# Sum over destinations in a graph network stack: loads of column pairs into eight buffers, landings passed on by GpSimd

## Chip, core and metric

The kernel runs on one core of a Trainium2 chip. The metric is the device time of one execution in microseconds (us). TensorE, VectorE, ScalarE and GpSimd (PE, DVE, ACT and POOL in the profile) compute; SyncE (SP) issues most transfers. Each engine runs its own instruction stream and waits on semaphores.

## What is computed

Four graph layers act on a state `x` of 1250 nodes by 768 features. There are 20,000 edges, sorted by destination, each with a relation from 34. The part that the change touches is in the second layer:

```python
agg  = segment_sum(x[src], edge_type * n + dst, num_segments=N_REL * n)
mean = agg / max(cnt, 1)
h1   = einsum('rni,rio->no', mean, W_rel) + x @ W_root + b_rgcn
xw   = h1 @ W_gcn
...            # the degree-normalised sum over edges, as in the other layers
```

The kernel does not form `mean`. It sorts the edges by relation, multiplies the gathered rows by the relation's weights, scales each by 1/count, and stores them in HBM as `messages`, one row of 768 floats per edge, in the order of the destinations. `h1` is then the sum of the messages by destination plus `x @ W_root + b_rgcn`.

## The kernel before

It is written out by hand: one program per engine, semaphores for every dependency, and hardware loops whose bounds are read from small tables that the kernel computes from the edges. The order on each engine is the order of the code.

At the start the edge lists are loaded and turned into `edge` (128 partitions by 160 columns: edge 128*j + p stands in column j, partition p). For each tile of 128 destination nodes VectorE computes the first column that holds one of its edges (`ctl_col`) and how many groups of four columns (a quad, `QUAD` = 4) the tile needs (`ctl_quad`, a running sum). With these inputs the ten tiles have 13, 6, 5, 4, 4, 3, 3, 3, 3 and 2 quads, so 52, 24, 20, 16, 16, 12, 12, 12, 12 and 8 columns, 184 in all. Then come the adjacency matrices, a normalisation, and the first layer's two convolutions (L0a and L0b). After them the relation stage gathers rows, multiplies and scatters `messages`.

The **sum stage** (`sum_tile` on each engine) follows. For tile t:

- TensorE transposes the tile of the state (L1240, from a copy in `rows`), and multiplies it by W_root in 36 products (L1249, `products`). Each fp32 operand is split into a high and a low part in fp32r, and three products of parts are summed.
- For each column j of the tile: SyncE loads 128 message rows into one of four buffers of `w_raw` (L502, 384 KB). ScalarE copies it as its high part into `y_part` (L817). VectorE writes the one-hot matrix of the column's destinations into one of four places of `agg_w` (L1205), and subtracts to get the low part (L1207). TensorE multiplies the one-hot with both parts in two halves, four matmuls into the tile's accumulator (L1417).
- After the last column VectorE adds the bias and writes the tile of `h_act` (L1212), and copies the tile after the next for the transposes (L1199).

The semaphores of a column: `Q.ylow` counts low parts, and the load that reuses a buffer waits for the low part four columns before. `y_land[k]` tells a landing, `Q.yhigh` a high part, and `Q.ymm` TensorE's columns. ScalarE and VectorE wait for `Q.ymm` before they overwrite a place used four columns before. TensorE and VectorE start the counts at `QUAD`, so the first four pass at once. `turn_low` (L856) takes the low part of the transposed tile, `quads` and `bounds` (L357 to L364) read the tables into registers, and `column` turns a quad and its place into j. The next layer's weights are loaded into `w_raw` when the last tile is added.

## Time and profile before

| | us |
|---|---|
| median of 3 runs | 3080.43 (3077.42 to 3080.8) |
| profiled execution, device time | 3085.96 |
| its span | 3084.0 |
| TensorE busy in the span | 2621.4 (85%) |
| VectorE busy | 1604.0 (52%) |
| ScalarE busy | 1126.3 (37%) |
| mean granted TensorE clock | 0.939 of 2.4 GHz |

Busy times are those of single engines, and they overlap. "Idle before" in a row is the time that the engine stood still ahead of the instruction, and the name after the arrow is what ended it. PEld is TensorE's weight load, which is ahead of the matmul that uses it. A line with a q after the engine (PEldq, DVEq) is an instruction of the engine's sequencer: register arithmetic, branches, waits.

### The profile page before, as it was taken

What the parts mean: (1) busy time and instruction counts of PE and PEld (TensorE: products, weight loads), DVE (VectorE), ACT (ScalarE), POOL (GpSimd) and SP (SyncE); (2) the same over time, 40 slices, a digit from 0 to 9 for tenths busy, and PEclk for the clock granted to TensorE, in tenths of its full rate; (3) what the DMA queues carried; (4) which work ended last, traced back from release to release, by engine and by line L of the source; (5) the groups of instructions that cost most, each with busy time, mean ns of one, the idle gap of its engine ahead of it and who ended that gap; (6) DMA issues with size and microseconds to landing.
All of it is one profiled execution on the core that took longest, in us unless ns stands there. A gap on an engine that the chain in (4) does not pass through costs nothing.

```text
span 3084.0 us, 52263 instructions
## 1 busy us (share of the span) xinstructions
PE 2621.4 (85%) x14502; PEld 2425.3 (79%) x14503; DVE 1604.0 (52%) x3028; ACT 1126.3 (37%) x1925; POOL 859.8 (28%) x1207
## 2 busy tenths in 40 slices
PE   0666388976999999999999999677778898987899
PEld 0222188976999999999999999556668887987799
DVE  7765543354344333443334433477764577577734
ACT  0011323232444444444444444355433235446521
POOL 1666610002555555555555555100000000000000
PEclk9987689998999999999999999889989998998999
DMA  3000110124445544555544554577660201001102
GB/s 108 1 1 1 44 47 0 45 86 169 175 174 182 196 174 174 174 188 190 174 174 172 195 188 143 184 239 228 207 199 21 77 25 36 10 13 69 51 21 91
DMA packets 116601, 358.08 MB, mean 116 GB/s; under 512 B 23709, under 2 KB 24177, under 8 KB 116337
## 3 DMA queue, kind: packets, MB, share of 16 engines
q1 hardware_dynamic: 78097, 220.40, 21.2%
q0 software_dynamic: 38464, 137.17, 12.8%
q8 instruction: 23, 0.38, 0.0%
q14 instruction: 17, 0.14, 0.0%
HBM read 267.97 MB, written 93.37 MB: 117 GB/s over the span
## 4 chain that ended last, share of the span: by engine, by line
PE 72%; DVE 11%; issue 5%; ACT 5%; DMA 4%; DVEq 2%; POOL 0%; ACTq 0%; SPq 0%; POOLq 0%
PE ps L1249 50%; PE ps L1304 12%; PE ps L1240 5%; PE ps L1356 4%; DMA w_raw<-messages 3%; DVE xw L1207 1%; PE ps L1417 1%; ACT xw L817 1%; DVE h_act L1115 1%; ACT rows L721 1%; DVE h_act L927 1%; DVEq L1113 1%; PE ps L1362 1%; DVE w_a L850 1%; DVE rows L981 1%
## 5 line engine op out<-in xcount | busy, mean ns | idle before, releaser
L1249 PE MATMUL ps<-w_a,h_t 128*128 128x384 f32 x5580 | 1032.3, 342 | 2.4 <-DVE h_t L856 2.1
L1249 PEld LDWEIGHTS ps<-w_a,h_t 128*128 128x128 f32 x5580 | 982.3, 192 | 6.9 <-DVE h_t L856 4.6
L1304 PE MATMUL ps<-xw,agg_w 128*128 128x384 f32 x2800 | 524.5, 350 | 78.8 <-DVE agg_w L952 47.2
L1304 PEld LDWEIGHTS ps<-xw,agg_w 128*128 128x128 f32 x2800 | 512.6, 197 | 87.7 <-issue 77.1
L1249 PE MATMUL ps<-xw,h_t 128*128 128x384 f32 x3132 | 577.4, 341 | 0.0
L1155 DVE TENSOR_TENSOR h_t<-ps,h_t 128x256 fp32r<-128x256 f32 x516 | 218.7, 424 | 678.5 <-ACT h_t L784 482.3
L1249 PEld LDWEIGHTS ps<-xw,h_t 128*128 128x128 f32 x3132 | 549.0, 188 | 0.0
L784 ACT ACTIVATE h_t<-ps 128x256 fp32r<-128x256 f32 x516 | 198.2, 384 | 677.2 <-PE ps L1249 472.0
L1240 PE MATMUL ps<-ident,rows 128*128 128x128 f32 x1458 | 206.8, 280 | 129.7 <-DVE rows L863 71.2
L636 POOL DMA_INDIRECT messages<-rows,rec_stage x172 | 199.9, 1162 | 354.1 <-ACT rows L778 354.1
L1240 PEld LDWEIGHTS ps<-ident,rows 128*128 128x128 f32 x1458 | 176.4, 144 | 146.3 <-issue 86.1
L599 POOL DMA_INDIRECT h_act<-h_table,rec_stage x175 | 188.7, 1078 | 147.1 <-POOL rec_stage L595 119.4
L1417 PE MATMUL ps<-xw,agg_w 128*128 128x384 f32 x736 | 178.2, 381 | 54.5 <-DVE xw L1207 50.0
L817 ACT ACTIVATE xw<-w_raw 128x768 fp32r<-128x768 f32 x184 | 152.6, 843 | 167.3 <-DMA w_raw<-messages 91.2
L1417 PEld LDWEIGHTS ps<-xw,agg_w 128*128 128x128 f32 x736 | 134.7, 206 | 95.9 <-DVE xw L1207 94.5
L1356 PE MATMUL ps<-h_act 128*128 128x512 bf16 x552 | 151.0, 393 | 63.1 <-DVE h_act L1115 53.6
L604 POOL DMA_INDIRECT w_at<-inv_table,rec_stage x175 | 182.9, 1045 | 61.4 <-issue 61.4
L1207 DVE TENSOR_TENSOR xw<-w_raw,xw 128x768 fp32r<-128x768 f32 x184 | 176.0, 957 | 44.4 <-ACT xw L817 43.7
L575 POOL DMA_INDIRECT records<-rec_stage x157 | 158.4, 1009 | 128.4 <-POOL rec_stage L571 121.7
L856 DVE TENSOR_TENSOR h_t<-ps,h_t 128x256 fp32r<-128x256 f32 x213 | 86.9, 423 | 185.6 <-ACT h_t L664 184.2
L1356 PEld LDWEIGHTS ps<-h_act 128*128 128x128 bf16 x552 | 43.4, 105 | 173.8 <-DVE h_act L1115 133.2
L664 ACT ACTIVATE h_t<-ps 128x256 fp32r<-128x256 f32 x183 | 70.2, 385 | 295.8 <-PE ps L1249 206.1
(183 smaller groups left out, 2188.8 us busy)
## 6 DMA issues: line engine op xcount, KB each, us to landing
w_raw<-in_L_gnn_W_rel SPq DMA_DIRECT2D x68, 1152.0 KB
w_raw<-messages SPq DMA_DIRECT2D x184, 384.0 KB, 3.8
rows<-x_state SPq DMA_DIRECT2D x50, 384.0 KB, 3.0
w_raw<-in_L_gnn_W SPq DMA_DIRECT2D x10, 1152.0 KB
x_state<-rows SPq DMA_DIRECT2D x30, 384.0 KB, 2.3
h_table<-h_act SPq DMA_DIRECT2D x10, 384.0 KB, 2.4
x_state<-in_x SPq DMA_DIRECT2D x1, 3750.0 KB, 14.2
out<-rows SPq DMA_DIRECT2D x9, 384.0 KB
```

Source lines behind the costliest of these rows:

```text
L599: pool.indirect_dma_start(out=x_ring[:, k, :], out_offset=None, in_=h_table, in_offset=bass.IndirectOffsetOnAxis(gather_at[:, k, 0:1], 0)) ...
L604: pool.indirect_dma_start(out=w_at[:, k:k + 1], out_offset=None, in_=inv_table, in_offset=bass.IndirectOffsetOnAxis(gather_at[:, k, 1:2], ...
L636: pool.indirect_dma_start(out=messages, out_offset=bass.IndirectOffsetOnAxis(scatter_at[:, k, :], 0), in_=rows[:, 2 + u, :], in_offset=Non ...
L784: act.activation(h_t[:, 0, 2 * g:2 * g + 2, :], turn_group(g).rearrange("p (k n) -> p k n", k=2), ACT.Copy)\
L817: act.activation(y_part[:, 0, k, :], w_raw[:, k, :], ACT.Copy).then_inc(Q.yhigh, 1)
L1155: dve.tensor_tensor(h_t[:, 1, 2 * g:2 * g + 2, :], turn_group(g).rearrange("p (k n) -> p k n", k=2), h_t[:, 0, 2 * g:2 * g + 2, :].bitcast ...
L1207: dve.tensor_tensor(y_part[:, 1, k, :], w_raw[:, k, :], y_part[:, 0, k, :].bitcast(F32), ALU.subtract)\
L1240: ins = pe.transpose(turn_out(k), tile[:, k * P:(k + 1) * P], ident[:])
L1249: ins = pe.matmul(acc(h), h_t[:, a, k, :], w[:, b, k, h * HF:(h + 1) * HF], start=(k == 0 and a == 0 and b == 0), stop=(stop and k == KB - ...
L1304: ins = pe.matmul(ps[:, 2 + 2 * u + h, 0:wide], agg_w[:, a, b, :], xw[:, c, b, h * HF:h * HF + wide], start=first, stop=last, skip_group_c ...
L1356: ins = pe.matmul(ps_flat[:, lo:hi], oh[:, k % 2, 0:P], oh[:, k % 2, P + lo:P + hi], start=False, stop=True, skip_group_check=True)
L1417: ins = pe.matmul(rel_acc(t)(h), agg_w[:, 0, k, :], y_part[:, b, k, h * HF:(h + 1) * HF], start=False, stop=True, skip_group_check=True)
```

## The change

In the sum stage:

- `w_raw` and `rows` become two parts of one tensor `land`, whose first eight rows of 768 floats are the landing buffers `y_ring`. `y_part` has eight places (`LAND` = 8) for each part. One load brings two columns (`PAIRS` = 4 loads in a round of eight columns).
- SyncE no longer follows the tiles: it loops over pairs of quads and reads each quad's first column from a table `quad_col`. The number of such pairs stands in `ctl_half[1]`. A load waits for the low parts of the two columns that were in its buffers, eight before.
- `quad_columns`, new on VectorE ahead of the relation stage, computes this table of 400 entries on one partition.
- GpSimd, after the relation stage, waits for each landing in turn and increments `Q.yready`. ScalarE waits for this count.
- ScalarE may be eight columns ahead of TensorE. The one-hots stay with VectorE and in four places: the counts start at `LAND`, and VectorE's wait is for four more than before.
- The places in `y_ring` and `y_part` are chosen by q % 2, a register value, where they were constants.
- The copy for the transposes of this stage goes to `rows[:, 2]`.

Elsewhere: six semaphores of the preparation become two counters, two become `x_ready`, and the rows of `messages` behind the last edge are zeroed with other shapes.

```diff
@@ constants, tensors
+LAND = 2 * QUAD
+PAIRS = LAND // 2
+    message_rows = messages[0:ECP * P, :].rearrange("(c p) d -> p c d", c=ECP)
-        w_raw = sb("w_raw", [P, KB, D], F32)
+        land = sb("land", [P, KB + 4, D], F32)
+        w_raw, rows = land[:, 0:KB, :], land[:, KB:KB + 4, :]
+        y_ring = land[:, 0:LAND, :]
-        rows = sb("rows", [P, 4, D], F32)
-        y_part = xw[:, :, 0:QUAD, 0:D]
+        y_part = xw[:, :, 0:LAND, 0:D]
+        quad_col = rec_out[0:1, :, :].rearrange("p c w -> p (c w)")[:, 0:QMAX]
+        quad_acc, quad_step = rows[0:1, 2, 0:QMAX], rows[0:1, 3, 0:QMAX]
+        def landed(q, k):
+            return y_ring[:, ds(q % 2 * QUAD + k, 1), :].rearrange("p a d -> p (a d)")
+        def part(a, q, k):
+            return y_part[:, a, ds(q % 2 * QUAD + k, 1), :].rearrange("p a d -> p (a d)")
@@ SyncE
-            at = E
-            while at < ECP * P:
-                n = min(ECP * P - at, 3 * 80)
-                sp.dma_start(messages[at:at + n, :].rearrange("(p r) d -> p r d", r=3), zero_rows[0:n // 3, :, :])\
-                  .then_inc(zeroed, 16)
-                at += n
+            sp.dma_start(message_rows[:, EC:ECP, :], zero_rows)\
+              .then_inc(x_ready, 16)
+            sp.dma_start(message_rows[ELAST:P, EC - 1:EC, :], zero_rows[ELAST:P, 0:1, :]).then_inc(x_ready, 16)
...
-            with sp.Fori(0, NT) as t:
-                q0, q1, c0 = quads(sp, t)
-                with sp.Fori(q0, q1) as q:
-                    for b in range(QUAD):
-                        j = column(c0, q, q0, b)
-                        sp.wait_ge(Q.ylow, q * QUAD + b + 1)
-                        sp.dma_start(w_raw[:, b, :], messages[ds(j * P, P), :])\
-                          .then_inc(y_land[b], 16)
+            pairs = sp.value_load(ctl_half[0:1, 1:2], min_val=1, max_val=QMAX // 2)
+            with sp.Fori(0, pairs) as i:
+                for u in range(2):
+                    j = sp.value_load(quad_col[0:1, ds(2 * i + u, 1)], min_val=0, max_val=ECP - QUAD)
+                    for b in range(2):
+                        k = 2 * u + b
+                        sp.wait_ge(Q.ylow, i * LAND + (2 * k + 2))
+                        sp.dma_start(y_ring[:, 2 * k:2 * k + 2, :], message_rows[:, ds(j + 2 * b, 2), :]).then_inc(y_land[k], 16)
+            for k in range(PAIRS):
+                sp.wait_ge(y_land[k], pairs * 16)
+                sp.sem_inc(turn_taken, 1)
@@ GpSimd, after the relation stage
+            pairs = pool.value_load(ctl_half[0:1, 1:2], min_val=1, max_val=QMAX // 2)
+            with pool.Fori(0, pairs) as i:
+                for k in range(PAIRS):
+                    pool.wait_ge(y_land[k], i * 16 + 16)
+                    pool.sem_inc(Q.yready, 1)
@@ ScalarE, sum_tile
-                        act.wait_ge(y_land[k], q * 16 + 16)
+                        act.wait_ge(Q.yready, q * 2 + (k // 2 + 1))
                         act.wait_ge(Q.ymm, q * QUAD + (k + 1))
-                        act.activation(y_part[:, 0, k, :], w_raw[:, k, :], ACT.Copy).then_inc(Q.yhigh, 1)
+                        act.activation(part(0, q, k), landed(q, k), ACT.Copy).then_inc(Q.yhigh, 1)
@@ VectorE
+            def quad_columns():
+                q_first, q_base, q_delta = att[0:1, 0, :], att[0:1, 1, :], seg_max[0:1, 0, :]
+                dve.wait_ge(R.addr, 1)
+                dve.tensor_copy(q_first, ctl_quad[0:1, 0:NT])
+                link(dve.tensor_copy(q_base, ctl_col[:]))
+                link(dve.scalar_tensor_tensor(q_base, q_first, -float(QUAD), q_base, ALU.mult, ALU.add))
+                dve.tensor_copy(q_delta[:, 0:1], q_base[:, 0:1])
+                dve.tensor_tensor(q_delta[:, 1:NT], q_base[:, 1:NT], q_base[:, 0:NT - 1], ALU.subtract)
+                link(dve.tensor_scalar(quad_acc, iota_n[0:1, 0:QMAX], float(QUAD), None, ALU.mult))
+                for t in range(NT):
+                    link(dve.tensor_scalar(quad_step, iota_n[0:1, 0:QMAX], q_first[:, t:t + 1], q_delta[:, t:t + 1],
+                                           ALU.is_ge, ALU.mult))
+                    link(dve.tensor_tensor(quad_acc, quad_acc, quad_step, ALU.add))
+                dve.tensor_scalar(mv[0:1, 0:1], ctl_quad[0:1, NT:NT + 1], 1.0, None, ALU.add)
+                link(dve.tensor_scalar(quad_col, quad_acc, float(ECP - QUAD), None, ALU.min))
+                link(dve.tensor_copy(ctl_half[0:1, 1:2], mv[0:1, 0:1]))
+                link(dve.tensor_scalar(ctl_half[0:1, 1:2], ctl_half[0:1, 1:2], 1, None, ALU.arith_shift_right))
+            quad_columns()
             dve.wait_ge(R.ready, 1)
...
-            dve.sem_inc(Q.ylow, QUAD)
+            dve.sem_inc(Q.ylow, LAND)
...
-                        dve.wait_ge(Q.ymm, q * QUAD + (k + 1))
+                        dve.wait_ge(Q.ymm, q * QUAD + (k + 1 + QUAD))
                         dve.tensor_scalar(agg_w[:, 0, k, :], iota_n[:, ds(t * P, P)], edge[:, 1, ds(j, 1)], None, ALU.is_equal)
                         dve.wait_ge(Q.yhigh, q * QUAD + (k + 1))
-                        dve.tensor_tensor(y_part[:, 1, k, :], w_raw[:, k, :], y_part[:, 0, k, :].bitcast(F32), ALU.subtract)\
+                        dve.tensor_tensor(part(1, q, k), landed(q, k), part(0, q, k).bitcast(F32), ALU.subtract)\
                            .then_inc(Q.ylow, 1)
@@ TensorE
-            pe.sem_inc(Q.ymm, QUAD)
+            pe.sem_inc(Q.ymm, LAND)
...
-                        pe.wait_ge(Q.ylow, q * QUAD + (k + 1 + QUAD))
+                        pe.wait_ge(Q.ylow, q * QUAD + (k + 1 + LAND))
                         for b in range(2):
                             for h in range(2):
-                                ins = pe.matmul(rel_acc(t)(h), agg_w[:, 0, k, :], y_part[:, b, k, h * HF:(h + 1) * HF],
+                                ins = pe.matmul(rel_acc(t)(h), agg_w[:, 0, k, :], part(b, q, k)[:, h * HF:(h + 1) * HF],
                                                 start=False, stop=True, skip_group_check=True)
```

On TensorE two columns of a quad in `sum_tile`'s inner loop stood like this (`xw` holds `y_part`, `sum_ylow` is `Q.ylow`, ISA is a register or wait instruction of the sequencer):

```order
L1417 MATMUL ps<-xw,agg_w 128x384 [waits sum_ylow]
L1417 MATMUL ps<-xw,agg_w 128x384 x3
L1414 REGISTER_ALU
L1417 MATMUL ps<-xw,agg_w 128x384 [waits sum_ylow]
L1417 MATMUL ps<-xw,agg_w 128x384 x3
```

and one column of the changed kernel, at the same place, stands like this:

```order
L1452 ISA [waits sum_ylow]
L1452 MATMUL ps<-xw,agg_w 128x384
L1452 ISA
L1452 MATMUL ps<-xw,agg_w 128x384
L1452 ISA
L1452 MATMUL ps<-xw,agg_w 128x384
L1452 ISA
L1452 MATMUL ps<-xw,agg_w 128x384
L1449 REGISTER_ALU
```

Each of the four matmuls of a column now has a sequencer instruction ahead of it, and the column's wait stands on the first of these.

On VectorE a column of the same loop stood so, the one-hot and the subtraction (`sum_ymm` is `Q.ymm`, `sum_yhigh` is `Q.yhigh`):

```order
L1205 ISA [waits sum_ymm]
L1205 ISA
L1205 TENSOR_SCALAR agg_w<-iota_n,edge 128x128
L1207 TENSOR_TENSOR xw<-w_raw,xw 128x768 [waits sum_yhigh]
L1204 REGISTER_ALU
```

and now:

```order
L1240 ISA [waits sum_ymm]
L1240 ISA
L1240 TENSOR_SCALAR agg_w<-iota_n,edge 128x128
L1241 REGISTER_ALU
L1242 ISA [waits sum_yhigh]
L1242 ISA
L1242 TENSOR_TENSOR xw<-land,xw 128x768
L1239 REGISTER_ALU
```

Three sequencer instructions have come between the one-hot and the subtraction.

On SyncE, which issues the loads, the inner loop of two columns stood so:

```order
L502 ISA [waits sum_ylow]
L502 DMA w_raw<-messages 128x768
L501 REGISTER_ALU
L502 ISA [waits sum_ylow]
L502 DMA w_raw<-messages 128x768
```

and half a round of the new loop, one quad, so:

```order
L505 TENSOR_LOAD rec_out
L505 ISA x2
L508 ISA
L509 ISA [waits sum_ylow]
L509 DMA land<-messages 128x2x768
L508 REGISTER_ALU
L509 ISA [waits sum_ylow]
L509 DMA land<-messages 128x2x768
```

A quad now takes two loads instead of four and one table read of its own (`quad_col` lies in `rec_out`); the reads of `ctl_quad` and `ctl_col` once a tile are gone.

## Rows read from the trace of the kernel before

**Rows 1.** The page, part 1: busy time, share of the span, instructions.

```profile
PE 2621.4 (85%) x14502; PEld 2425.3 (79%) x14503; DVE 1604.0 (52%) x3028; ACT 1126.3 (37%) x1925; POOL 859.8 (28%) x1207
```

**Rows 2.** Groups by line, 1966 to 2298 us: busy, mean ns, idle before.

```profile
L1207 DVE TENSOR_TENSOR xw<-w_raw,xw 128x768 fp32r<-128x768 f32 x184 | 176.0, 957 | 44.4 <-ACT xw L817 43.7
L817 ACT ACTIVATE xw<-w_raw 128x768 fp32r<-128x768 f32 x184 | 152.6, 843 | 167.3 <-DMA w_raw<-messages 91.2 <-PE ps L1417 70.8 <-issue 1.9
```

**Rows 3.** Waits, 1966 to 2298 us: total, times, longest.

```profile
PEld ps L1417 <- DVE xw L1207: 94.5, 122, 1.8
ACT xw L817 <- DMA w_raw<-messages: 91.2, 109, 2.4
...
DVE agg_w L1205 <- PE ps L1417: 30.8, 10, 4.8
```

**Rows 4.** Timeline of VectorE, 2049 to 2070 us: start, duration, instruction, idle before.

```profile
2051.77 0.96 DVE L1212 TENSOR_TENSOR h_act<-ps,rows 128x768 f32 x1 [1.36 <-PE ps L1417]
...
2063.05 0.29 DVE L1205 TENSOR_SCALAR agg_w<-iota_n,edge 128x128 fp32r x1 [3.69 <-PE ps L1417]
2063.58 0.96 DVE L1207 TENSOR_TENSOR xw<-w_raw,xw 128x768 fp32r<-128x768 f32 x1 [0.24 <-ACT xw L817]
...
2064.65 0.95 DVE L1207 TENSOR_TENSOR xw<-w_raw,xw 128x768 fp32r<-128x768 f32 x1
```

**Rows 5.** Timeline of TensorE and its weight loads, second and fourth tile.

```profile
2053.89 8.08 PE L1249 MATMUL ps<-w_a,h_t 128*128 128x384 f32 x36
...
2061.63 3.61 PEld L1417 LDWEIGHTS ps<-xw,agg_w 128*128 128x128 f32 x20
2065.66 0.65 PEld L1417 LDWEIGHTS ps<-xw,agg_w 128*128 128x128 f32 x4 [0.41 <-DVE xw L1207]
...
2131.15 6.49 PE L1249 MATMUL ps<-w_a,h_t 128*128 128x384 f32 x36
```

**Rows 6.** Timeline of VectorE, first restart, end of the second tile, last addition.

```profile
1978.23 0.29 DVE L1205 TENSOR_SCALAR agg_w<-iota_n,edge 128x128 fp32r x1 [4.18 <-PE ps L1417]
...
2091.28 0.95 DVE L1207 TENSOR_TENSOR xw<-w_raw,xw 128x768 fp32r<-128x768 f32 x1
...
2093.61 0.96 DVE L1212 TENSOR_TENSOR h_act<-ps,rows 128x768 f32 x1 [0.39 <-PE ps L1417]
...
2296.10 0.96 DVE L1212 TENSOR_TENSOR h_act<-ps,rows 128x768 f32<-128x768 f32 x1 [1.06 <-PE ps L1417]
```

**Rows 7.** Stretches: length, busy by engine, TensorE clock, DMA share, GB/s.

```profile
1963.00:1964.00 1.00, 0.00 (x0) 0.00 (x0) 0.00 (x0) 0.00 (x0) 0.00 (x0) 0.50 1.03 402
...
1975.00:1976.00 1.00, 1.00 (x8) 1.00 (x7) 0.00 (x0) 0.00 (x0) 0.00 (x0) 1.00 0.87 304
...
1978.00:2048.00 70.00, 49.97 (x195) 35.98 (x193) 53.36 (x95) 39.70 (x48) 0.00 (x0) 0.90 0.79 247
```

**Rows 8.** DMA issues of the stage: KB each, median us to landing.

```profile
w_raw<-messages SPq DMA_DIRECT2D x184, 384.0 KB, 3.8
```

**Rows 9.** Sequencer instructions of lines: min/median/max ns, first and last start.

```profile
L1414 PEldq ALU_OP  x3: 32/32/36, 2287.1 to 2287.7; - x3
...
L1249 PEldq FUSED_REGOPS  x362: 60/91/136, 743.7 to 2257.4; - x181
...
L1205 DVEq FUSED_REGOPS  x228: 52/158/231, 1969.3 to 2293.0; - x114
```

**Rows 10.** Timeline, 725 to 742 us: GpSimd and VectorE.

```profile
725.89 0.11 POOL L589 MEMSET rows<- 128x10 int32 x1 [320.95 <-DMA h_table<-h_act]
...
740.90 0.56 DVE L1167 COPY rows<-h_act 128x768 f32<-128x768 f32 x1 [18.50 <-POOLq L612]
```

**Rows 11.** Timelines of VectorE at the start and in the first layer.

```profile
48.04 0.18 DVE L1068 TENSOR_SCALAR rows<-rows 128x34 f32<-128x34 f32 x1
48.26 0.19 DVE L1069 TENSOR_TENSOR rows<-rows 128x33 f32<-128x33 f32 x1
...
721.72 0.68 DVE L915 TENSOR_SCALAR h_act<-rows,mv 128x768 f32<-128x768 f32 x1
```

More of the change, by code:

```diff
@@ L338, in gnn_stack @@
         Q = SumSems(sem)
-        y_land = [sem(f"y_land{b}") for b in range(QUAD)]
+        y_land = [sem(f"y_land{b}") for b in range(PAIRS)]
         block = ctx.enter_context(nc.Block())
@@ L1198, in sum_tile @@
                     dve.wait_ge(Q.turned, KG * t + KG)
-                    dve.tensor_copy(rows[:, 0, :], tile_rows(h_act, t + 1)).then_inc(Q.copied, 1)
+                    dve.tensor_copy(rows[:, 2, :], tile_rows(h_act, t + 1)).then_inc(Q.copied, 1)
                 q0, q1, c0 = quads(dve, t)
@@ L1328, in _ @@
                 ins = pe.transpose(ps[:, 1, a * 32:(a + 1) * 32], float_b[:, a, :], ident[0:32, 0:32])
-            ins.then_inc(pre.turned, 1)
-            pe.wait_ge(pre.extremes, 1)
-            pe.transpose(ps[0:2 * NT, 2, 0:P], small[:, 0, 0:2 * NT], ident[:]).then_inc(pre.extremes_turned, 1)
-            pe.wait_ge(pre.best, 1)
+            ins.then_inc(pre.pe_step, 1)
+            pe.wait_ge(pre.dve_step, 1)
+            pe.transpose(ps[0:2 * NT, 2, 0:P], small[:, 0, 0:2 * NT], ident[:]).then_inc(pre.pe_step, 1)
+            pe.wait_ge(pre.dve_step, 2)
             pe.matmul(ps[0:1, 3, 0:2 * NT], small[0:2 * NT, 1, 0:1], ident[0:2 * NT, 0:2 * NT], start=True, stop=True)\
-              .then_inc(pre.row, 1)
-            pe.wait_ge(pre.tot, 1)
+              .then_inc(pre.pe_step, 1)
+            pe.wait_ge(pre.dve_step, 3)
             own = small[:, 3, 0:NR]
             pe.matmul(ps[:, 4, 0:NR], before[:], own, start=True, stop=True, skip_group_check=True)
-            pe.matmul(ps[:, 4, 64:64 + NR], ones[:], own, start=True, stop=True, skip_group_check=True).then_inc(pre.prefix, 1)
+            pe.matmul(ps[:, 4, 64:64 + NR], ones[:], own, start=True, stop=True, skip_group_check=True).then_inc(pre.pe_step, 1)
             cuts = [(0, 512), (512, 1024), (1024, NP + NR)]
@@ L1397, in _ @@
             pe.wait_ge(w_low, 2 * (w_no["root"] + 1))
-            pe.sem_inc(Q.ymm, QUAD)
+            pe.sem_inc(Q.ymm, LAND)
             pe.wait_ge(Q.copied, 1)
-            turn(Q, rows[:, 0, :])
+            turn(Q, rows[:, 2, :])
             def sum_tile(t, more):
@@ L1405, in sum_tile @@
                     pe.wait_ge(Q.copied, t + 2)
-                    turn(Q, rows[:, 0, :])
+                    turn(Q, rows[:, 2, :])
                 pe.wait_ge(Q.ofree, t + 1)
```

43 lines of the change are left out of this document (19 added, 24 removed).

## Prediction

> **What bounds the kernel now.** I read the page's first part, then by stretch. Over the whole span TensorE is busy for 85% [rows 1], but the diff works in one stage, the sum over destinations, which runs here from about 1960 to 2297 us. In that stage the groups by line and the waits show something else than the page: TensorE, VectorE and ScalarE all wait in turn. ScalarE's split L817 waits 91.2 us for landings of column loads, TensorE's weight load waits 94.5 us for VectorE's low part L1207, and VectorE's one-hot waits 30.8 us in ten pieces for TensorE [rows 2, 3]. Followed back: TensorE waits for VectorE, VectorE for ScalarE, ScalarE for a load whose buffer was freed only four columns before.
>
> The timeline of VectorE shows two kinds of time. When columns have landed, low parts follow each other every 1.07 us (2063.58, 2064.65): a one-hot and a subtraction. After a tile's last column comes a pause of another kind: the addition to `h_act`, the copy for the next transposes, four columns ahead, and then a stop until TensorE has done the root products and one column; for the second tile it runs from 2051.77 to 2063.05 [rows 4]. TensorE itself needs only 0.72 us for a column at 2.4 GHz (20 weight loads, so five columns, in 3.61 us) and 6.5 us for the root products, 8.1 us when part of them falls on 1.2 GHz [rows 5].
>
> So there are 184 columns, and three rates: VectorE 1.07 us, TensorE 0.72 us, and what the loads give. From the first restart of VectorE (1978.23) to the last addition (2296.10) are 317.9 us [rows 6]. The nine pauses from a tile's addition to the next restart, 7.8 to 12.4 us long, make 94.3 us of it (the first is that of [rows 4], 11.3). The other 223.6 us are column stretches, and in them loads set the rate: 1.48 us a column in the first tile of 52.
>
> **The change part by part.**
>
> *Eight landing and eight part buffers, loads of pairs.* Loads run eight columns ahead, ScalarE eight columns ahead of TensorE. The one-hots still have four places, and the wait for them is shifted so that it remains "TensorE has done the column four before". The pauses therefore stay as they are, and a column stretch becomes VectorE's own pace if loads keep up. A tile of n columns then takes, from its restart: 0.2 us to the first subtraction, (n-5) times 1.066, and 2.33 from the last subtraction's start to the addition (2091.28 to 2093.61, a tile whose last columns ran at 2.4 GHz) [rows 6]. The tiles have 52, 24, 20, 16, 16, 12, 12, 12, 12 and 8 columns, so n-5 adds up to 134: 134 x 1.066 + 10 x 2.53 = 168.1 us. Against 223.6 that is a gain of **55.4 us**, 20.9 of it in the first tile.
>
> *Do the loads keep up?* One column is 393 KB. With loads queued behind each other the engines moved 402 GB/s, 0.98 us a column; four single loads spaced by VectorE got 304 GB/s, 1.29 us; the present stretch 247 GB/s at a DMA share of 0.79, which is latency (median 3.8 us to landing, four buffers) more than rate [rows 7, 8]. Pairs, four of them in the queue, stand between the first two; I take 1.15 us. In the first tile that is 48 x (1.15 - 1.066) = 4.0 us, against at least four columns landed when the stretch starts, so 0 to 4: I take 2. At 1.29 it is 48 x 0.22 = 10.8 less some 4.3 of store, and little in the 24-column tile: 7. At 0.98 nothing. The Trainium skill ("DMA: Bandwidth & Descriptors", section Measured) puts a 1 MB transfer at 341 GB/s, and the section on 436 GB/s sees an HBM limit of about 358 per core. By those a column would take 1.10 to 1.15 us, loads and not VectorE would be the pace, and the first tile would lose 1.6 to 4 us, by an estimate from that page. The trace's 402 GB/s is above it.
>
> *Slots addressed by register.* ScalarE, VectorE and TensorE now compute addresses before each instruction. On VectorE one such step takes 0.05 to 0.23 us, median 0.16 [rows 9]. In the steady state they run while a 0.96 us subtraction does, and three or four of them fit into 1.066. Only at a restart nothing covers the two ahead of the subtraction: 0.2 us ten times, **-2.0 us**. On TensorE four steps come per column. Its sequencer passed three columns' loop steps between 2287.1 and 2287.7, some 0.3 us for four weight loads and matmuls [rows 9]. A step of TensorE's costs 0.06 to 0.14 us, median 0.09 [rows 9], so a column needs 0.3 + 4 x 0.09 = 0.66 us of sequencer, still under 0.72. At 0.136 it is 0.84, still under 1.066. What is exposed is the first step after each release, at a tile's last column: 0.15 us ten times, **-1.5 us**. ScalarE has 0.84 us of work against 1.066 and is ahead by up to eight.
>
> *GpSimd passes landings on.* One more semaphore step per pair. From the end of a low part (2064.65 + 0.95) to TensorE's weight load at 2065.66 are 0.06 us [rows 4, 5], so the hop costs about 0.1 to 0.2 us in landing time. GpSimd has nothing else left to do then, and with a pair in store it is hidden: 0. If loads set the pace it lies in their loop of eight columns and is worth 0.02 us a column.
>
> *The table of columns.* `quad_columns` puts 29 small instructions on VectorE ahead of the relation stage, released by the memset at 725.89; VectorE would start there at 740.90 [rows 10]. Nothing of 1 x 400 elements is in the trace. Scaling between 33 and 768 elements, a tensor-tensor goes from 0.19 to 0.96, so 0.57 at 400; a tensor-scalar from 0.18 to 0.68, so 0.43 [rows 11, 2]. Ten pairs with 0.04 between are 10.8 us, the rest some 2.3: 13.1 us in a gap of 14.9. The cover is GpSimd's records load and first gather. If every tensor-scalar cost as much as a tensor-tensor it would be 14.8: 0. If an instruction took 20% more than that, 3 us would be exposed on the chain (TensorE idles there too).
>
> *The rest.* Fewer semaphores and another cut of the zeroing at the start: the same 480 rows, waited for hundreds of microseconds later: 0. The load of the next weights still follows the last addition. The first loads are now eight columns behind the load of `h_act`; with one queue in order that load is not later.
>
> *TensorE's clock.* In the first stretch its mean grant is 0.90 [rows 7]: short spells at 1.2 GHz while it waits much. With a column per 1.07 us instead of 1.48 it waits less. The five slow pauses of 11.2 us or more could come down to the 9.7 of the fast ones (up to +9 us); against it, a spell at 1.2 GHz inside a stretch, where a column takes about 1.37 us, now costs 0.3 us a column, where loads covered it before. I take **+2 us**.
>
> Sum: 55.4 - 2.0 - 2.0 - 1.5 + 2 = 51.9. The profiled execution took 3085.96 us (span 3084.0), so 3034 for it; the median of the runs shown is 5.5 us lower, 3080.43, so I forecast **3029 us**.
>
> **The rivals.**
>
> *Loads set the pace* (0.16). If pairs get no more than 1.4 to 1.5 us a column, as the stretch does now, the first tile costs some 20 - 5, the next two 4 more: 20 us off the sum, gain 32, 3048. For it: today's 247 GB/s at a share of 0.79. Against it: 402 GB/s while queued.
>
> *TensorE's instruction stream becomes the pace* (0.09). If a column needs c of sequencer above 0.95 us, the stage takes 184 c + 86.8 (94.3 less ten times 0.75 for what lies between TensorE's first column and VectorE's restart). At c = 1.19 (0.147 per matmul and 0.15 per step) that is 305.8 against 317.9: gain 12, 3068. Against it: 0.3 us for four matmuls now.
>
> *Slower* (0.03). The same mechanism on the other side: it decides from c = 1.256, that is 0.31 us for each matmul with its address step. At c = 1.4 the stage takes 344 us, 27 more: 3107. The Trainium skill ("TensorE: Matmul & The Clock Gate", section "Wait — 56ns, not 53.3ns?") gives about 62 ns a matmul where ucode decodes it. The row's pace for weight load and matmul together agrees roughly with that, so this stays small.
>
> *It does not do what it says* (0.03): the four one-hot places tie VectorE to TensorE, so buffers behind them could be worth nothing, 3080. Against it: the one-hot waits only 30.8 us, all of it in the pauses [rows 3].
>
> *More than forecast* (0.07): no shortfall of loads and all pauses fast, gain 60 to 64, 3017 to 3020.
>
> **How the numbers follow.** My forecast, VectorE's pace with a gain of 42 to 60, has 0.62; its own range is 3020 to 3039. The range of 3017 to 3054 adds the higher gain and loads as the pace, and leaves out about 0.15. Slower by over 0.2% is 0.03, within 0.2% 0.03 (about what a measurement of this kernel can tell from no change), faster 0.94.
>
> **What would show it.** In the changed profile: ScalarE's wait for landings falls from 91 to under 15 us, low parts every 1.07 us from restart to tile end, waits of VectorE for TensorE still ten and some 30 us, first tile 53 to 58 us instead of 73.5, the last addition near 2244. Steps within TensorE's column: weight loads of a column in 0.65 us as now; if they spread to 1 us or more, the forecast is wrong by the second rival. If landings still release ScalarE in the first tile, it is the first. VectorE starting the relation stage later than 740.9 would show the table exposed.

## The result, and the profile after

| | before | after |
|---|---|---|
| median | 3080.61 us | 3038.27 us |
| ratio after to before (95% interval) | | 0.9861 (0.9842 to 0.988) |
| profiled execution | 3085.96 us | 3035.31 us |
| span | 3084.0 us | 3033.2 us |
| granted TensorE clock, mean | 0.939 | 0.943 |

One more execution of each kernel was disturbed and some 800 to 1000 us longer; the ratio leaves both out, and without them the medians are 3080.43 and 3038.12 us. The change makes the kernel 1.4% faster: 42.3 us by the medians and 50.7 us between the two profiled executions. Forecast were 3029 us, and a range of 3017 to 3054 that holds the result; it lies at the upper edge of the main forecast's own range, 3020 to 3039. The difference between 42 and 51 is itself a part of the answer, below.

The groups by line of the sum stage of the changed kernel, 1960 to 2262 us (line, engine, instruction, busy us, mean ns, idle before and what ended it). They answer to [rows 2]; the one-hot is now L1240, the low part L1242, ScalarE's split L832, TensorE's column L1452.

```profile
L1242 DVE TENSOR_TENSOR xw<-land,xw x184 | 175.6, 954 | 9.0 <-ACT xw L832 5.5 <-issue 0.4
L1452 PE MATMUL ps<-xw,agg_w 128*128 x736 | 167.5, 357 | 20.4 <-DVE xw L1242 9.6
L832 ACT ACTIVATE xw<-land x184 | 144.7, 837 | 119.9 <-POOLq L660 85.1 <-PE ps L1452 33.8 <-issue 0.8
L1452 PEld LDWEIGHTS ps<-xw,agg_w 128*128 128x128 f32 x736 | 121.9, 188 | 64.5 <-issue 64.4
...
L1240 DVE TENSOR_SCALAR agg_w<-iota_n,edge 128x128 fp32r (+1 forms) x184 | 51.9, 282 | 40.6 <-PE ps L1452 22.2 <-issue 18.3
```

The subtraction takes what it took, 954 ns. What has gone is the idle time around it: VectorE waits 5.5 us for ScalarE in the whole stage, ten times (before 43.7). Two rows must be read with care. ScalarE still waits 85.1 us for landings, nearly as long as before, but now it stands up to eight columns ahead, and only those 5.5 us of it reach VectorE. And TensorE's weight load no longer shows "VectorE" as the end of its 64.4 us but "issue": its wait for the low part stands on the register step ahead of the first weight load now, and the profile can't follow a semaphore through that.

VectorE's timeline in the first tile (start, duration, instruction, idle before):

```profile
1989.91 0.96 DVE L1242 TENSOR_TENSOR xw<-land,xw  x1
1990.78 0.28 DVE L1240 TENSOR_SCALAR agg_w<-iota_n,edge 128x128 fp32r x1
1990.98 0.95 DVE L1242 TENSOR_TENSOR xw<-land,xw  x1
1991.85 0.28 DVE L1240 TENSOR_SCALAR agg_w<-iota_n,edge 128x128 fp32r x1
1992.49 0.96 DVE L1242 TENSOR_TENSOR xw<-land,xw  x1 [0.36 <-ACT xw L832]
```

Low parts start 1.07 us apart, as forecast, and now and then one is late because its pair hasn't landed: seven waits of 0.27 to 0.75 us in this tile. The first eight steps behind the restart are all 1.07 us, and the ninth is the first late one; from there to the end of the tile the mean is 1.19 us. The first restart and the last addition, for the length of the stage, and the first tile's end with the restart behind it:

```profile
1976.28 0.29 DVE L1240 TENSOR_SCALAR agg_w<-iota_n,edge 128x128 fp32r x1 [4.15 <-PE ps L1452]
...
2034.06 0.96 DVE L1247 TENSOR_TENSOR h_act<-ps,land 128x768 f32 x1 [0.46 <-PE ps L1452]
...
2045.37 0.29 DVE L1240 TENSOR_SCALAR agg_w<-iota_n,edge 128x128 fp32r x1 [3.48 <-PE ps L1452]
...
2242.72 0.96 DVE L1247 TENSOR_TENSOR h_act<-ps,land 128x768 f32<-128x768 f32 x1 [1.17 <-PE ps L1452]
```

From 1976.28 to 2242.72 are 266.4 us. The stage before took 317.9, and 317.9 less the forecast gain of 51.9 is 266.0. Cut as in the prediction: nine pauses of 88.0 us together (before 94.3) and ten stretches of 178.5 (before 223.6). The first tile takes 57.8 us instead of 73.5. The tiles of 8, 12 and 16 columns take 5.74, 10.3 and 14.6 us, with no wait for a load in them.

TensorE's register steps, in the sequencer's rows (ns: shortest, median, longest), answer to [rows 9]:

```profile
L1452 PEldq FUSED_REGOPS  x736: 46/46/120, 1973.8 to 2242.0; - x184
```

and the table, VectorE from the memset on:

```profile
724.23 0.11 POOL L598 MEMSET land<- 128x10 int32 x1 [321.71 <-DMA h_table<-h_act]
...
725.37 0.47 DVE L1173 TENSOR_SCALAR land<-iota_n,att,seg_max 1x400 f32<-1x400 uint16 x1
725.88 0.56 DVE L1175 TENSOR_TENSOR land<-land 1x400 f32<-1x400 f32 x1
...
737.08 0.14 DVE L1179 TENSOR_SCALAR ctl_half<-ctl_half 1x1 int32<-1x1 int32 x1
739.95 0.56 DVE L1202 COPY land<-h_act 128x768 f32<-128x768 f32 x1 [2.73 <-POOLq L621]
```

It ends 12.8 us after it started (forecast 13.1, with 29 instructions where there are 30), and VectorE then waits 2.73 us for the first gather: the table is hidden. The relation stage starts 15.7 us after the memset, before it was 15.0 [rows 10]. The difference of 0.7 us was 0.5 between x_before and x_after. VectorE waits for GpSimd in all four profiles, so the table doesn't end that wait, and why GpSimd is later is not shown.

### The profile page after: what moved, and what is told of

Same layout as the page of the kernel before. It is cut to its first block, busy times and chain, and to the rows that moved or that the text cites. A ratio compares the mean times of both kernels' runs of the same rounds, so it can differ in the third digit from the quotient of the medians.

```text
span 3033.2 us, 53789 instructions
## 1 busy us (share of the span) xinstructions
PE 2610.2 (86%) x14502; PEld 2412.2 (80%) x14503; DVE 1604.6 (53%) x3058; ACT 1118.5 (37%) x1925; POOL 857.5 (28%) x1207
## 4 chain that ended last, share of the span: by engine, by line
PE 76%; DVE 10%; ACT 4%; issue 4%; DMA 2%; DVEq 2%; POOL 1%; ACTq 0%; SPq 0%; POOLq 0%
PE ps L1284 51%; PE ps L1339 12%; PE ps L1275 5%; PE ps L1391 4%; PE ps L1452 3%; DMA land<-messages 1%; DVE h_act L1130 1%; DVE h_act L942 1%; ACT land L736 1%; PE ps L1397 1%; DVE w_a L865 1%; DVEq L1128 1%; DVE land L996 1%; DVE land L955 1%; DVE xw L1242 0%
## 5 line engine op out<-in xcount | busy, mean ns | idle before, releaser
L1339 PE MATMUL ps<-xw,agg_w 128*128 128x384 f32 x2800 | 528.7, 351 | 78.3 <-DVE agg_w L967 47.0
L1339 PEld LDWEIGHTS ps<-xw,agg_w 128*128 128x128 f32 x2800 | 516.8, 198 | 87.2 <-issue 77.4
L1275 PE MATMUL ps<-ident,land 128*128 128x128 f32 x1458 | 206.9, 280 | 129.7 <-DVE land L878 70.8
L645 POOL DMA_INDIRECT messages<-land,rec_stage x172 | 200.3, 1164 | 349.3 <-ACT land L793 349.3
L1275 PEld LDWEIGHTS ps<-ident,land 128*128 128x128 f32 x1458 | 177.3, 144 | 143.8 <-issue 57.8
L832 ACT ACTIVATE xw<-land x184 | 144.7, 837 | 119.9 <-POOLq L660 85.1
L1452 PE MATMUL ps<-xw,agg_w 128*128 x736 | 167.5, 357 | 20.4 <-DVE xw L1242 9.6
L1242 DVE TENSOR_TENSOR xw<-land,xw x184 | 175.6, 954 | 9.0 <-ACT xw L832 5.5
L1452 PEld LDWEIGHTS ps<-xw,agg_w 128*128 128x128 f32 x736 | 121.9, 188 | 64.5 <-issue 64.4
```

What stands on the lines that cost most here:

```text
L645: pool.indirect_dma_start(out=messages, out_offset=bass.IndirectOffsetOnAxis(scatter_at[:, k, :], 0), in_=rows[:, 2 + u, :], in_offset=Non ...
L1242: dve.tensor_tensor(part(1, q, k), landed(q, k), part(0, q, k).bitcast(F32), ALU.subtract)\
L1275: ins = pe.transpose(turn_out(k), tile[:, k * P:(k + 1) * P], ident[:])
L1339: ins = pe.matmul(ps[:, 2 + 2 * u + h, 0:wide], agg_w[:, a, b, :], xw[:, c, b, h * HF:h * HF + wide], start=first, stop=last, skip_group_c ...
L1452: ins = pe.matmul(rel_acc(t)(h), agg_w[:, 0, k, :], part(b, q, k)[:, h * HF:(h + 1) * HF], start=False, stop=True, skip_group_check=True)
```

## The experiments

All kernels are edits of the changed kernel unless said otherwise. Each ratio is against executions of before taken beside it. Their median was 3082.52 us beside x_before, x_after, x_ahead4 and x_single, 3085.88 beside x_hop, x_table2, x_hot8 and x_quad, and 3080.92 beside x_ahead6, x_single4 and x_hot8_single, so medians of different groups are compared only to a few us. "Stage", "pauses" and "stretches" are cut as above, from the profiled execution of each. "Pace" is that of the first tile, (its time - 2.83) / 47: the 2.83 us are what a tile takes besides the n - 5 columns (0.42 from the restart to the first low part and 2.41 from the last one's start to the addition). For before it is 2.6. Where one-hots have eight places VectorE doesn't stop after four columns, and the stage is counted from the fifth one-hot all the same.

**x_before, x_after: both kernels again.** No edit.

> The kernel before, profiled a second time. Theory A (the first profiled execution stood some 5 us above the median because TensorE's clock fell more often in the pauses between tiles): this one takes about 3080, and its nine pauses of the sum stage add up to 86 to 91 us instead of 94.3; the column stretches stay at 220 to 225 us. Theory B (the 5 us were spread over the whole span, outside the stage): pauses again 94 us, and the stage from first restart to last addition again 318 us.

> The changed kernel again, with more rounds. If the stage's gain of 51.5 us between the two profiles is the gain of the change, the time is 48 to 52 us under the kernel before; if part of it was the first profile of the kernel before, 40 to 46 us under it. Stage 264 to 270 us from first restart to last addition.

Before again: 3077.98 us, stage 308.1, pauses 86.3, stretches 221.8. After again: 3037.51 us, ratio 0.9845 (0.9825 to 0.9865), stage 266.2, pauses 86.3, stretches 179.9. Between these two profiled executions the whole difference is 40.5 us and that of the stage 41.9, all of it in stretches. So in the first profile of before 8 us were slow pauses that another execution does not have, and the change does nothing to pauses.

**x_single: eight single loads.** One load per column, each with its own semaphore; GpSimd passes on each.

```diff
-                        sp.wait_ge(Q.ylow, i * LAND + (2 * k + 2))
-                        sp.dma_start(y_ring[:, 2 * k:2 * k + 2, :], message_rows[:, ds(j + 2 * b, 2), :]).then_inc(y_land[k], 16)
+                        sp.wait_ge(Q.ylow, i * LAND + (k + 1))
+                        sp.dma_start(y_ring[:, k:k + 1, :], message_rows[:, ds(j + b, 1), :]).then_inc(y_land[k], 16)
```

> The changed kernel with eight loads of one column each in the eight places instead of four pairs. Theory 1 (depth): first tile within 3 us of the changed kernel's 57.8, time within 4 us of it; perhaps a little better, since a place is refilled one column earlier. Rival (pairs raise the rate of the loads): first tile 62 to 70 us, time 6 to 20 us slower than the changed kernel.

3029.64 us, ratio 0.9824 (0.9809 to 0.984). Stage 259.2, pauses 88.0, stretches 171.2, first tile 52.9. That is neither of the expected cases: singles are 7.9 us faster than x_after, outside the 4 us of the first theory, and the rival had the wrong sign. The rows of the stage, and below them the stretch 1985 to 2017 us (busy by engine, then clock, DMA share, GB/s):

```profile
L1242 DVE TENSOR_TENSOR xw<-land,xw x184 | 174.8, 950 | 3.3 <-ACT xw L832 0.4 <-issue 0.3
...
1985.00:2017.00 32.00, 29.09 (x122) 19.62 (x122) 32.00 (x61) 23.93 (x29) 0.00 (x0) 1.00 0.99 358
```

VectorE is busy for all 32 us and waits 0.4 us for ScalarE in the stage: this is VectorE's pace without a shortfall, 1.065 us a column. So the forecast's figure for a stage with loads that keep up is right (its 168.1 us plus 3.0 of register steps, below), and pairs cost 8.7 us of stretches against singles (179.9 to 171.2).

**x_quad: two loads of four columns**, the other way.

```diff
+                    sp.wait_ge(Q.ylow, i * LAND + (QUAD * u + QUAD))
+                    sp.dma_start(y_ring[:, QUAD * u:QUAD * u + QUAD, :], message_rows[:, ds(j, QUAD), :]).then_inc(y_land[u], 16)
```

> The changed kernel with two loads of four columns (1.5 MB each) in a round of eight instead of four pairs. Theory (rate is not the limit, the loop from a freed place to its landing is): coarser refills make the store give out earlier: first tile 60 to 72 us, 4 to 20 us slower. Rival (larger loads move at the 400 GB/s of queued ones and that is what limits): first tile 53 to 57 us and 2 to 6 us faster.

3083.58 us, ratio 0.9992 (0.9982 to 1.0002). Stage 309.5, stretches 220.2, first tile 74.8: eight buffers as in the change, and the whole gain is gone, far more than the 4 to 20 us expected. VectorE's timeline and the same stretch:

```profile
1989.77 0.96 DVE L1240 TENSOR_TENSOR xw<-land,xw  x1 [3.94 <-ACT xw L830]
...
1995.72 0.96 DVE L1240 TENSOR_TENSOR xw<-land,xw  x1 [1.59 <-ACT xw L830]
...
2002.06 0.96 DVE L1240 TENSOR_TENSOR xw<-land,xw  x1 [1.99 <-ACT xw L830]
```

```profile
1985.00:2017.00 32.00, 21.62 (x77) 17.30 (x77) 20.86 (x39) 15.23 (x20) 0.00 (x0) 0.77 0.75 260
```

Four columns come at once and then VectorE waits 2 us, every 6.3 us. The DMA engines are busy for 75%, not full.

**x_ahead4, x_ahead6, x_single4: the ring held to fewer columns.** The load waits for a low part four, two and four columns later; the last with single loads.

```diff
-                        sp.wait_ge(Q.ylow, i * LAND + (2 * k + 2))
+                        sp.wait_ge(Q.ylow, i * LAND + (2 * k + 2 + 4))    # x_ahead4; x_ahead6: + 2
-                        sp.wait_ge(Q.ylow, i * LAND + (k + 1))            # of x_single
+                        sp.wait_ge(Q.ylow, i * LAND + (k + 1 + 4))        # x_single4
```

> The changed kernel with loads let out only four columns ahead of the low parts, still in pairs and in eight places. Theory 1 (the gain is the depth of eight columns in landing buffers): the gain is lost and more, since two pairs in flight are coarser than four single loads: first tile 72 to 85 us, time 0 to 25 us above the kernel before. Rival (the gain comes from pairs, fewer issues, or from ScalarE and the parts being eight deep): the first tile stays under 65 us and most of the 42 us remain.

> Pairs as in the change, each waiting for a low part two columns later: six columns ahead instead of eight. With four ahead the stretches took 299.6 us, with eight 179.9. Theory A (a ring turns in a fixed time from a freed pair to its landing and split, so the pace is that time over the columns ahead; from four ahead: 98.4 / 52 = 1.89 us a column, 7.6 us a turn, of which six ahead would give 1.26): first tile 63 to 68 us, stretches 195 to 210, 3055 to 3070 us. Rival B (the 8 us that pairs cost at eight ahead is a loss at the tile's start, not a pace, and six ahead is still enough): stretches 180 to 186, 3037 to 3044 us.

> Single loads, but each waits for a low part four columns later, so that only four columns are ahead as in the kernel before; the eight places, register steps, the pass through GpSimd and the table stay. Theory A (the gain of the change is the depth of the load ring and nothing else; the other parts cost next to nothing): stretches 220 to 226 us as before (221.8), pauses 86 to 90, 3078 to 3086 us. Rival B (part of the gain comes from elsewhere, for instance from fewer semaphores or ScalarE's eight part buffers): stretches under 215 us, under 3070. Rival C (the hop and the register steps, which eight columns of store hide, show once the loads set the pace): four columns per turn of the ring and 0.1 to 0.3 us a turn more, 46 turns: stretches 226 to 236, 3086 to 3096.

x_ahead4: 3158.36 us, ratio 1.0252 (1.0236 to 1.0267), stage 387.9, stretches 299.6, first tile 98.4: 76 us over before, where 0 to 25 were expected. x_ahead6: 3071.89 us, 0.9975 (0.9962 to 0.9988), stretches 209.8, first tile 66.1, in the expected window but for a time just above it. x_single4: 3090.33 us, 1.0034 (1.002 to 1.0047), stretches 233.8, first tile 76.2, which is the third of its cases. From x_single it differs in the wait alone, and this is worth 62.6 us of stretches (233.8 to 171.2): the depth of the ring is the gain. The 12 us over x_before's 221.8, 0.26 us per turn of four columns, are what the pass through GpSimd, the register steps and the new loop on SyncE cost together when loads set the pace; they were not taken apart. With eight single loads none of it is seen.

Median times from a load's issue to its landing, in the issue rows of x_single, x_single4, x_ahead6, the changed kernel and x_quad, in this order (each from its own profile):

```profile
land<-messages SPq DMA_DIRECT2D x184, 384.0 KB, 4.5
```

```profile
land<-messages SPq DMA_DIRECT2D x184, 384.0 KB, 3.8
```

```profile
land<-messages SPq DMA_DIRECT2D x92, 768.0 KB, 4.6
```

```profile
land<-messages SPq DMA_DIRECT2D x92, 768.0 KB, 5.4
```

```profile
land<-messages SPq DMA_DIRECT2D x46, 1536.0 KB, 6.5
```

Put together, after the runs, one relation fits all of them roughly. A load of g columns in a ring of A is issued when the *last* of its g places is free, and lands as a whole for its *first* column. That leaves it A - g + 1 columns of lead (landing times of before and of x_ahead4 are from issue rows not shown, that of x_after is from its own profile, not the one above):

| kernel | A | g | lead, columns | pace, us a column | landing, us |
|---|---|---|---|---|---|
| x_ahead4 | 4 | 2 | 3 | 2.03 | 4.4 |
| before (x_before) | 4 | 1 | 4 | 1.50 | 3.8 |
| x_single4 | 4 | 1 | 4 | 1.56 | 3.8 |
| x_quad | 8 | 4 | 5 | 1.53 | 6.5 |
| x_ahead6 | 6 | 2 | 5 | 1.35 | 4.6 |
| the change (x_after) | 8 | 2 | 7 | 1.18 | 5.7 |
| x_single | 8 | 1 | 8 | 1.065, VectorE's | 4.5 |

In a steady ring, lead times pace less the subtraction's 0.96 us must cover landing and split. For x_ahead6 that is 5 x 1.35 - 0.96 = 5.8 us against 4.6 + 0.84 = 5.4; for before 5.0 against 4.6, for x_ahead4 5.1 against 5.2, for x_quad 6.7 against 7.3, for x_single4 5.3 against 4.6. It is an estimate to 0.8 us. For x_after it gives (5.7 + 0.84 + 0.96) / 7 = 1.07 us, right at VectorE's 1.066, so that every late pair shows; measured were 1.18. For eight singles it gives 0.79, and a late load is covered. Lead alone doesn't order the kernels: x_quad has 5 columns and is no faster than before with 4; its loads take 6.5 us to land and not 3.8. Nor is the landing time a constant of the load: the same pairs land in 4.4 us with four columns ahead, in 4.6 with six and in 5.4 to 5.7 with eight.

**x_hop: the pass through GpSimd made longer.** Two reads of the table between landing and increment.

```diff
                     pool.wait_ge(y_land[k], i * 16 + 16)
+                    pool.sem_inc(turn_taken, 1)
+                    for _ in range(2):
+                        pool.value_load(ctl_half[0:1, 1:2], min_val=1, max_val=QMAX // 2)
                     pool.sem_inc(Q.yready, 1)
```

> The changed kernel with two table reads on GpSimd between each landing and its increment, about 1 us more for every pair. Theory (the hop lies in the loop of loads only where the store of landed columns has run out): 10 to 12 us of delay do not show in the short tiles; the first tile grows by 3 to 8 us and the time by 4 to 12 us. Rival (the hop is on every pair's path): 92 times 1 us in part, 40 us or more. Rival (the hop is nowhere on the path): within 2 us.

The sequencer's rows of that line give the price of one read:

```profile
L662 POOLq FUSED_REGOPS  x176: 147/147/152, 1980.0 to 2250.8; - x176
L662 POOLq SEQ_ASSERT  x176: 18/18/18, 1980.1 to 2251.0; - x176
L662 POOLq TENSOR_LOAD <-ctl_half x175: 282/286/305, 1980.2 to 2250.5; - x175
```

Two of 0.45 us are 0.90 us more per pair. 3053.36 us, ratio 0.9899 (0.9878 to 0.9919). Stretches 187.9 against 179.9: 8.0 us, 4.1 in the first tile, whose pace goes from 1.177 to 1.264. With a lead of 7 the relation above gives 0.90 / 7 = 0.13, and 0.09 were found. So where loads are tight a column pays for the pass, but less than a seventh of its delay. In the changed kernel GpSimd's own step for a pair is one wait of 17 ns:

```profile
L660 POOLq EVENT_SEMAPHORE  x92: 17/17/17, 1963.8 to 2234.5; - x92
```

What a semaphore's way from one engine to the next adds is not in this row. At the 0.1 to 0.2 us of the prediction the pass would cost 1 to 2 us of stretches, an estimate by the 8.0 us for 0.90. With 1.7 us of pauses the stage is 9.8 us longer than x_after's; the medians are 15.8 us apart, 12.5 if each is taken from before beside it, where 4 to 12 were expected. Another 6 us of the profiled executions lie in the relation stage (first restart less relation start is 1239.9 us here, 1234.0 in x_after), whose code is the same; the kernels with four one-hot places have 1233.6 to 1240.0 there, so I take it as that stage's own spread; its cause is not shown. The profiled execution won back 3.5 us elsewhere.

**x_table2: the table computed twice.**

```diff
             quad_columns()
+            quad_columns()
```

> The changed kernel with the table of columns computed twice, 12.8 us more of VectorE ahead of the relation stage. Theory (the first 12.8 us are covered with some 2.7 us to spare): the relation stage starts about 10 us later and the time grows by 9 to 11 us. Rival (what was covered is only partly so): 12 to 13 us. Rival (the cover is longer than the idle row shows): under 6 us.

3051.99 us, ratio 0.9887 (0.9867 to 0.9907), 14.5 us over x_after, or 11.1 if each is taken from before beside it (33.9 under it, x_after 45.0); expected were 9 to 11. The relation stage starts 26.0 us after the memset and not 15.7:

```profile
752.24 0.14 DVE L1179 TENSOR_SCALAR ctl_half<-ctl_half 1x1 int32<-1x1 int32 x1
752.42 0.56 DVE L1203 COPY land<-h_act 128x768 f32<-128x768 f32 x1
```

With two tables VectorE goes on without a wait, and what stands beyond the old start is lost whole: 10.3 us. The single table had 2.7 us of cover left. The profiled execution (3056.43 us) is 18.9 us over x_after's: the others are 6.0 in the relation stage and 3.4 in pauses, both of which vary with the execution.

**x_hot8: the one-hots in eight places too.** `hot_place` picks one of eight by q % 2; VectorE waits for TensorE's column eight before. TensorE takes one of two bodies with fixed addresses, by q % 2.

```diff
-                        dve.wait_ge(Q.ymm, q * QUAD + (k + 1 + QUAD))
-                        dve.tensor_scalar(agg_w[:, 0, k, :], ...)
+                        dve.wait_ge(Q.ymm, q * QUAD + (k + 1))
+                        dve.tensor_scalar(hot_place(q, k), ...)
@@ TensorE
+                    with pe.If(q % 2 < 1):
+                        quad_products(0)
+                    with pe.If(q % 2 > 0):
+                        quad_products(1)
```

> The changed kernel with one-hots in eight places as well: VectorE's wait is then for TensorE's column eight before; TensorE chooses between two written-out quads by a branch, so its addresses are constants. Theory (the pauses are TensorE's root products plus VectorE standing still after four columns): VectorE's 22 us of waits for TensorE go, and 1.9 to 4.2 us a tile are gained, less where the loads give out earlier: 10 to 20 us faster than the changed kernel, 3018 to 3028. Rival (loads set the pace once VectorE works through the pause): under 6 us faster, and ScalarE's waits for landings grow by what VectorE's waits shrink.

3019.21 us, ratio 0.9795 (0.9776 to 0.9814). The stage is 253.8 us, 12.4 shorter than x_after's: pauses 69.4 instead of 86.3, stretches 184.4 instead of 179.9. VectorE spends less time standing, and the loads have less time to build up a store; with single loads the stretches don't grow (next run). The medians are 18.3 us apart, so some 6 us of that are not in the stage as it is counted here, where each of the restarts is set at the fifth one-hot.

**x_hot8_single: both.**

> The eight single loads and the eight places of the one-hots together. Theory A (the two act on different things: single loads bring the column stretches to VectorE's pace, eight one-hot places take the wait for TensorE out of the pauses): the stage from VectorE's first restart to the last addition takes 69 us of pauses plus about 175 to 177 of stretches, 244 to 247, and the run 3009 to 3014 us, some 8 below eight places with pairs (3019.2). First tile 53 to 55 us. Rival B (once the one-hots run ahead, VectorE or TensorE's register steps and not the loads make the 4.9 us by which those stretches were longer than with four places): stretches stay at 182 to 185, 3017 to 3020 us.

3007.12 us, ratio 0.9762 (0.974 to 0.9783), the fastest kernel of the study: 2.4% under before. Stage 240.4, pauses 69.5, stretches 170.9; the two act apart, as the first theory had it, and the stage comes out below its 244. From 1985 to 2017 us its DMA engines moved 363 GB/s at a share of 1.00, so little is left there for a faster VectorE:

```profile
1985.00:2017.00 32.00, 29.03 (x127) 20.44 (x126) 32.00 (x62) 24.71 (x30) 0.00 (x0) 1.00 1.00 363
```

A pause of this kernel, VectorE:

```profile
2027.77 0.96 DVE L1251 TENSOR_TENSOR h_act<-ps,land 128x768 f32 x1 [0.36 <-PE ps L1457]
2028.65 0.55 DVE L1238 COPY land<-h_act 128x768 f32 x1
2031.21 0.29 DVE L1244 TENSOR_SCALAR agg_w<-iota_n,edge  x1 [2.01 <-issue]
2031.50 0.96 DVE L1246 TENSOR_TENSOR xw<-land,xw  x1
...
2034.70 0.96 DVE L1246 TENSOR_TENSOR xw<-land,xw  x1
2035.57 0.28 DVE L1244 TENSOR_SCALAR agg_w<-iota_n,edge  x1
2035.77 0.95 DVE L1246 TENSOR_TENSOR xw<-land,xw  x1
```

In [rows 4] VectorE stopped after four columns until TensorE was through with the root products. Here it goes on with the fifth, at 2035.57. The 2.01 us ahead of the first one-hot stay; they are the loop bounds of the next tile, read from the tables.

## Why the prediction was right, and where it was not

**What sets the pace: right.** VectorE at 1.07 us a column wherever columns have landed, its waits for TensorE in the pauses left as they were (22.2 us in nine here and 20.0 in nine in x_after, 30.8 in ten in the first profile of before and 22.5 in ten in x_before), TensorE's own stream not in the way. A column's four weight loads take 0.65 us as before, and one register step 46 ns at the median, not 0.09 us:

```profile
1979.94 0.65 PEld L1452 LDWEIGHTS ps<-xw,agg_w 128*128 128x128 f32 x4 [0.41 <-issue]
```

TensorE's weight loads stand idle for 0.41 us between two columns. That rules out the second rival and the slower one, which both needed a stream above 0.95 us a column. "It does not do what it says" fell with the result.

**Exposed register steps (-2.0 and -1.5): right in sum, 3.0 us.** The short tiles have no load in their way and show it: 5.74 us for 8 columns and 10.30 for 12 are 0.42 + (n - 5) x 1.066 + 2.41 to 0.3 us. Forecast without the steps were 0.2 and 2.33. So a tile costs 0.3 us more, ten of them 3.0, of the 3.5: 0.22 at the restart (forecast 0.2) and 0.08 at the end (forecast 0.15). The 0.2 was a steady column's figure and not one of a restart. Before took 0.53 from restart to subtraction, 0.24 of it a wait for ScalarE [rows 4], and the changed kernel takes 0.42.

**Do the loads keep up (-2): the step that failed.** The stretches came to 178.5 us. Less 134 x 1.066 + 28.3 = 171.1 that is 7.4 us of shortfall, 4.9 of it in the first tile, 1.3 in each of the next two. x_single, with a shortfall of 0.1, shows that it comes from the loads. The forecast took a cost per column from rates, and its 1.15 us was nearly met: the first tile's pace here is 1.17 (57.78 less 2.83, over 47). What was mis-sized is what it took off. It let the store halve the first tile's 4.0 us, and it put the two tiles behind at nothing, which cost 2.6 us. The store did carry eight steps, and the pace behind it was 1.19. The rival of loads at 1.4 to 1.5 us a column, as before, did not come.

That the 1.15 was close is luck in part, since it was read from rates. The 402 GB/s of a full queue stood in a stretch of 1 us, and no 32 us listed here have more than 363. From 1985 to 2017 us eight singles move 358 GB/s at a DMA share of 0.99 and pairs 334 at 0.96; from 1977 to 2009 both have a share of 0.88, singles 313 and pairs 299 GB/s. The changed kernel's two stretches, and below them x_single's of 1977 to 2009:

```profile
1977.00:2009.00 32.00, 27.28 (x116) 18.61 (x115) 30.07 (x56) 18.91 (x25) 0.00 (x0) 1.00 0.88 299
1985.00:2017.00 32.00, 26.23 (x109) 17.57 (x108) 29.32 (x55) 20.81 (x27) 0.00 (x0) 1.00 0.96 334
...
1977.00:2009.00 32.00, 29.48 (x129) 20.94 (x128) 29.91 (x56) 21.61 (x26) 0.00 (x0) 1.00 0.88 313
```

These shares don't tell whether the engines could have done more for pairs. x_hop does in part: 0.90 us of delay that moves no bytes costs 0.09 us a column, some 0.6 us of the seven columns' lead, so the time from a freed pair to its landing is for the most part what sets the pace. The lead explains it: a pair waits for its second place and holds up its first column, and x_quad, at a share of 0.75, takes that to where nothing of the gain is left. That the size of the load plays a part beside the lead is not excluded: no run holds single loads to a lead of 7. The value for "at 1.29" in the prediction, 7, is what it came to, by another way. The Trainium skill ("DMA: Bandwidth & Descriptors", section Measured) gives larger transfers the higher rate, for transfers issued from GpSimd, and by it singles should have been the slowest form. Here, with rings of the same eight buffers and loads issued from SyncE, it was the other way: 358 GB/s with 384 KB, 334 with 768 KB, 260 with 1.5 MB, all from 1985 to 2017 us.

**TensorE's clock and the pauses (+2): right in sign for the first pair of profiles, and nothing in general.** Between those the pauses came down by 6.3 us. x_before had 86.3 us of pauses without the change, x_after 86.3 with it. The slow pauses of 11.2 us and more (two in the changed kernel's profile, five in before's) come and go with the execution, so the sign was luck. The spells at 1.2 GHz inside a stretch that were set against it did not come in the part looked at: the granted clock is 1.00 from 1977 to 2017 us.

**From the profile to the median: the other term that was off.** The forecast of 3034 us for the profiled execution was missed by 1.3 us; in the stage a shortfall of 5.4 more was made up by 4.3 of pauses and 0.5 of steps, so that nearness is luck. Then 5.5 us were taken off, since the profiled execution of before was that much above its median. But part of what made it longer were five slow pauses, and the changed kernel's execution had only two. Reckoned to typical executions, the gain is 55.4 - 7.4 - 3.0, less the 1.8 by which x_before's stretches were shorter than the first profile's: 43.2 us, and 41.9 were found in the stage. The runs don't resolve more: the five later runs put the ratio at 0.9825 to 0.9865, which is 42 to 54 us.

**The table and the pass through GpSimd (0 and 0): right**, both by cover. The table's 12.8 us are hidden with 2.7 to spare and would cost in full behind that (x_table2). Nothing is seen of the pass with eight single loads; with pairs it may be worth 1 to 2 us (estimate, x_hop), and together with the register steps and SyncE's loop it is 12 us when only four columns are ahead (x_single4).

**ScalarE's wait for landings: a wrong sign to look for.** "Under 15 us" was expected and 85.1 came. The engine runs ahead of what it feeds, so its wait says only that it is the faster one. What it passes on is VectorE's wait for it, 5.5 us. In x_single, where no load is short, ScalarE still waits 68.5 us for landings and VectorE 0.4 for ScalarE.

## What to carry to other kernels

Reckon a ring of buffers by its lead, ring size less columns per load plus one, times the pace of the consumer, and hold that against the time from issue to landing plus the steps behind it: a bigger load in the same ring takes lead away, and small loads with enough in flight can be the faster ones. The landing time has to be that of the ring reckoned with, since it grew here with the columns in flight. When an engine ahead of the pace-setter waits, follow the wait to the next engine before counting it as a loss. And before a gain in waits is forecast from one profile, see whether another execution has these waits at all.

## What the runs showed of the hardware that was not expected

- A matmul whose operand's place is picked by a register has a step of 46 ns ahead of its weight load (median of 736), and four of them leave the 0.65 us of a column's weight loads unchanged.
- From 1985 to 2017 us, four 384 KB loads in flight with 3.8 us to landing give 251 to 261 GB/s (x_single4, both profiles of before) and eight give 358 GB/s at 4.5 us; four of 768 KB give 334 at 5.4 us, two of 1.5 MB 260 at 6.5 us.
- One `value_load` on GpSimd, from a table in on-chip memory, takes 0.45 us of its sequencer (147 + 18 + 286 ns).
- From the start of the relation stage to VectorE's first restart in the sum stage, code that is the same in all kernels here, it took from 1233.6 to 1240.0 us in the executions profiled (kernels with four one-hot places).
